# The first layer's 780 pairs in six full row groups, and the last 34 of them stacked three times in the seventh

## The reference

```
x0 = xk = e                                   # (1024, 39, 16)
for W in (f0, f1, f2):                        # (39*39,128), (128*39,128), (128*39,128)
    z = einsum('bfd,bgd->bfgd', x0, xk).reshape(b, f * g, d)
    xk = einsum('bpd,pm->bmd', z, W)          # (b, 128, 16)
    outs.append(xk)
h = concat(sum(concat(outs, 1), -1), dense_ctx)   # (1024, 400)
y = relu(relu(h @ W_top1 + b1) @ W_top2 + b2) @ W_top3
```

## Time and profile before

| | |
|---|---|
| median of 3 runs | 1332.29 us (1331.56 to 1333.27) |
| the profiled execution's own time | 1330.08 us |
| its span, first to last instruction | 1328.3 us |
| mean granted TensorE clock | 0.992 of full speed |
| busy shares PE / DVE / ACT / POOL | 96% / 87% / 69% / 79% |

### The profile page before, as it was taken

The page is one execution under the profiler, slowest core; times in us unless marked ns, Lnnn a source line. Parts: engine busy times, 40 slices in busy tenths (PEclk is TensorE's granted clock), DMA queues, the critical chain, the costliest instruction groups (busy, mean ns, idle before and its releaser), DMA issues. The chain is left out here.

```text
span 1328.3 us, 21624 instructions
## 1 busy us (share of the span) xinstructions
PE 1276.6 (96%) x5983; PEld 1015.4 (76%) x5983; DVE 1155.5 (87%) x3210; ACT 915.7 (69%) x3053; POOL 1050.0 (79%) x743
## 2 busy tenths in 40 slices
PE   4799999999999999999999999999999999999998
PEld 2487777887778777887778877788777877788787
DVE  3499999699988999789996999969999799988983
ACT  2377776577766777677775777757776677767783
POOL 7588888688886888779887788968888688884661
PEclk9799999999999999999999999999999999999999
DMA  7732333322333332223333033331233322223000
GB/s 192 163 58 53 61 64 65 62 38 47 53 62 62 64 58 43 47 52 62 66 64 59 10 64 66 64 62 15 57 64 65 62 54 44 45 57 62 1 3 1
DMA packets 129421, 76.08 MB, mean 57 GB/s; under 512 B 90792, under 2 KB 98201, under 8 KB 129301
## 3 DMA queue, kind: packets, MB, share of 16 engines
q1 hardware_dynamic: 119061, 72.07, 26.6%
q0 software_dynamic: 10240, 2.64, 2.3%
HBM read 68.16 MB, written 3.87 MB: 54 GB/s over the span
## 5 line engine op out<-in xcount | busy, mean ns | idle before, releaser
L392 ACT ACTIVATE parts<-pieces,x_cols 128x128 f32<-128x128 f32 x2560 | 718.1, 377 | 166.1 <-PE pieces L688 164.0
L526 DVE SCALAR_TENSOR_TENSOR parts<-pieces,x_cols,parts 128x128 f32<-128x128 f32 x2432 | 679.4, 340 | 113.2 <-PE pieces L688 92.0
L686 PE MATMUL pieces<-w_hi,cur_hi 128*128 128x512 f32 (+1 forms) x1280 | 548.1, 428 | 22.4 <-DVE parts L526 22.2
L688 PE MATMUL pieces<-w_hi,cur_lo 128*128 128x512 f32 (+1 forms) x1280 | 498.6, 390 | 0.0
L687 PE MATMUL pieces<-w_lo,cur_hi 128*128 128x512 f32 (+1 forms) x1280 | 498.4, 389 | 0.0
L340 POOL TENSOR_TENSOR parts<-parts 128x1024 f32<-128x1024 f32 x127 | 320.3, 2522 | 140.0 <-DVE parts L526 136.8
L331 POOL DMA_INDIRECT emb<-in_table,rows x320 | 342.2, 1069 | 80.8 <-issue 62.1
L686 PEld LDWEIGHTS pieces<-w_hi,cur_hi 128*128 128x128 f32 x1280 | 241.5, 189 | 93.5 <-DVE parts L526 43.8
L411 ACT ACTIVATE pairs_hi<-pairs 117x512 fp32r<-117x512 f32 (+1 forms) x224 | 141.9, 634 | 202.2 <-DVE pairs L536 192.2
L688 PEld LDWEIGHTS pieces<-w_hi,cur_lo 128*128 128x128 f32 x1280 | 240.9, 188 | 51.5
L687 PEld LDWEIGHTS pieces<-w_lo,cur_hi 128*128 128x128 f32 x1280 | 242.0, 189 | 47.7
(11 more groups left out here) (66 smaller groups left out, 596.4 us busy)
## 6 DMA issues: line engine op xcount, KB each, us to landing
partners<-x_wide SPq DMA_DIRECT2D x62, 546.0 KB
partners<-x_wide SPq DMA_DIRECT2D x31, 468.0 KB
x_rep<-x_wide SPq DMA_DIRECT2D x96, 78.0 KB
emb<-in_table,rows POOLq DMA_INDIRECT x320
x_diag<-x_cols SPq DMA_DIRECT2D x256, 10.0 KB
x_wide<-emb SPq DMA_DIRECT2D x32, 80.0 KB
x_wide<-emb SPq DMA_DIRECT2D x32, 32.0 KB
wt<-in_wt SPq DMA_DIRECT2D x1, 1024.0 KB
```

Source lines behind the costliest of these rows:

```text
L392: last = nc.scalar.activation(parts[n % 2][:, 4 * i + r, :], src[:, r * H:(r + 1) * H], ACT.Copy, scale=x_cols[n // 4][:, n % 4, f:f + 1])
L526: nc.vector.scalar_tensor_tensor(acc, src[:, r * H:(r + 1) * H], x_cols[n // 4][:, n % 4, f:f + 1], acc, ALU.mult, ALU.add).then_inc(acc_d ...
L686: nc.tensor.matmul(dst[:, 0:width], hi[:, cols], w1_hi[:, ws], start=True, stop=False)
L688: nc.tensor.matmul(dst[:, 0:width], lo[:, cols], w1_hi[:, ws], start=False, stop=True).then_inc(l2d_ready if q in D_PIECES else l2a_ready, 1)
```

## The change

The pairs are laid out anew. Groups 1 to 6 have all 128 rows: 117 as before (three shifts), and 11 more rows (SPARE) with pairs of fields 0 to 10 of a further shift. That holds 746 different pairs (repeats have zero weights), and 34 are left. They go into a group of 40 rows (10 fields by 4 shifts, with some repeats whose weights are zero), and the 40 rows stand three times in the seventh group (120 rows). In the first 40 rows the operands are the high parts, in the next 40 high pairs by low weights, in the last 40 low pairs by high weights, so one product (L670's place) gives what three gave. For this the seventh group's low-part instruction on DVE becomes a `scalar_tensor_tensor`, which takes the high part away only in rows 80 to 119 by a factor per partition (`take_low`), and the weights of the group are built likewise. The seventh group multiplies by a new tile `x_end`. `load_x` now issues 7 transfers and `load_partners` 7, where each issued 3; the waits count them. The weights come in two transfers, zeros included, where there were five and a memset; `shift_rows` has 128 rows a group.

```diff
@@ -35,14 +35,16 @@
 
 REP = 3
 FX = F + 1
-KPART = REP * F
-
-SHIFTS = F // 2 + 1
-PAIRK = (SHIFTS + REP - 1) // REP
-LAST_ROWS = (SHIFTS - REP * (PAIRK - 1)) * F
+SPARE = P - REP * F
+PAIRK = 7
+FULL = PAIRK - 1
+WHOLE_SHIFTS = REP * FULL
+END_FIELDS, END_SHIFTS = 10, 4
+END = END_FIELDS * END_SHIFTS
+LAST_ROWS = REP * END
 XT_ROWS = 2 * F
 X_STEP = XT_ROWS
-X_LOADS, WIDE_STORES, DIAG_LOADS = 1, 3, BLK_B
+X_LOADS, PARTNER_LOADS, WIDE_STORES, DIAG_LOADS = REP + 1 + REP, REP + 1 + REP, 3, BLK_B
 
 PIECES = 10
...
@@ -81,7 +83,7 @@
 
 
 def rows_of(k):
-    return KPART if k < PAIRK - 1 else LAST_ROWS
+    return P if k < FULL else LAST_ROWS
 
 
 def cin_kernel(nc, t, out):
...
@@ -233,16 +236,9 @@
                 sp.dma_start(part, t["w1"][cols, :].rearrange("(f g) m -> g f m", g=H)).then_inc(w1_loaded, 16)
             sp.dma_start(ident[:], t["ident"]).then_inc(const_loaded, 16)
             sp.dma_start(shift_rows, t["shift_rows"]).then_inc(const_loaded, 16)
-            whole = KPART * (PAIRK - 1)
-            sp.dma_start(w0_raw[:, 0:PAIRK - 1, :],
...
-            sp.dma_start(w0_swapped[:, 1:PAIRK - 1, :], t["w0_swapped"][KPART - F:whole - F, :].rearrange(
-                "(k p) m -> p k m", p=KPART)).then_inc(w0_loaded, 16)
-            sp.dma_start(w0_swapped[0:LAST_ROWS, PAIRK - 1, :], t["w0_swapped"][whole - F:, :]
-                         ).then_inc(w0_loaded, 16)
+            sp.dma_start(take_low[:], t["take_low"]).then_inc(const_loaded, 16)
+            sp.dma_start(w0_raw, t["w0"].rearrange("(k p) m -> p k m", p=P)).then_inc(w0_loaded, 16)
+            sp.dma_start(w0_swapped, t["w0_swapped"].rearrange("(k p) m -> p k m", p=P)).then_inc(w0_loaded, 16)
 
             def store_tile(tile, i):
...
@@ -267,13 +263,25 @@
                 first = x_wide[bass.ds(tile, 1), 0:F, :].rearrange("o r c -> (o r) c")
                 for r in range(REP):
                     sp.dma_start(x_rep[i % 2][r * F:(r + 1) * F, :], first).then_inc(x_rep_loaded[i % 2], 16)
+                sp.dma_start(x_rep[i % 2][REP * F:P, :], first[0:SPARE, :]).then_inc(x_rep_loaded[i % 2], 16)
+                end = first[SPARE:SPARE + 1, :]
+                src = bass.AP(end.tensor, end.offset, [[0, END_SHIFTS], [COLS, END_FIELDS], [1, COLS]])
+                for r in range(REP):
+                    sp.dma_start(x_end[i % 2][r * END:(r + 1) * END, :], src).then_inc(x_rep_loaded[i % 2], 16)
 
             def load_partners(tile, i):
+                flat = x_wide[bass.ds(tile, 1), :, :]
                 for r in range(REP):
-                    steps = len(range(r, SHIFTS, REP))
-                    first = x_wide[bass.ds(tile, 1), r:r + F, :].rearrange("o r c -> (o r) c")
-                    src = bass.AP(first.tensor, first.offset, [[COLS, F], [REP * COLS, steps], [1, COLS]])
-                    sp.dma_start(partners[i % 2][r * F:(r + 1) * F, 0:steps, :], src
+                    src = bass.AP(flat.tensor, flat.offset + r * COLS, [[COLS, F], [REP * COLS, FULL], [1, COLS]])
+                    sp.dma_start(partners[i % 2][r * F:(r + 1) * F, 0:FULL, :], src
+                                 ).then_inc(partners_loaded[i % 2], 16)
+                src = bass.AP(flat.tensor, flat.offset + WHOLE_SHIFTS * COLS,
+                              [[COLS, SPARE], [COLS, FULL], [1, COLS]])
+                sp.dma_start(partners[i % 2][REP * F:P, 0:FULL, :], src).then_inc(partners_loaded[i % 2], 16)
+                src = bass.AP(flat.tensor, flat.offset + (SPARE + WHOLE_SHIFTS) * COLS,
+                              [[COLS, END_SHIFTS], [COLS, END_FIELDS], [1, COLS]])
+                for r in range(REP):
+                    sp.dma_start(partners[i % 2][r * END:(r + 1) * END, FULL, :], src
                                  ).then_inc(partners_loaded[i % 2], 16)
 
...
@@ -459,9 +467,8 @@
                 last = nc.scalar.activation(w1_hi[:, cols], part.rearrange("p f m -> p (f m)"), ACT.Copy)
             last.then_inc(w1_hi_ready, 1)
             act.wait_ge(w0_summed, 1)
-            nc.scalar.activation(w0_hi[:, 0:PAIRK - 1, :], w0_raw[:, 0:PAIRK - 1, :], ACT.Copy)
-            nc.scalar.activation(w0_hi[0:LAST_ROWS, PAIRK - 1, :], w0_raw[0:LAST_ROWS, PAIRK - 1, :], ACT.Copy
-                                 ).then_inc(w0_hi_ready, 1)
+            nc.scalar.activation(w0_hi[:, 0:FULL, :], w0_raw[:, 0:FULL, :], ACT.Copy)
+            nc.scalar.activation(w0_lo[:, FULL, :], w0_raw[:, FULL, :], ACT.Copy).then_inc(w0_hi_ready, 1)
             act.wait_ge(ones_set, TILES)
             copy_x_cols(0, 0)
             for k in range(PAIRK):
...
+                                (tile - i % 2) * 8 * PARTNER_LOADS + i % 2 * 16 * PARTNER_LOADS)
                 wait(dve, pairs_lo_ready, g - 1)
-                nc.vector.tensor_tensor(pairs[buf][0:rows, :], partners[i % 2][0:rows, k, :], x_rep[i % 2][0:rows, :],
+                x = x_rep[i % 2] if k < FULL else x_end[i % 2]
+                nc.vector.tensor_tensor(pairs[buf][0:rows, :], partners[i % 2][0:rows, k, :], x[0:rows, :],
                                         ALU.mult).then_inc(pairs_ready, 1)
 
...
 
             def take_pairs_low(tile, i, k):
                 g, buf, rows = tile * PAIRK + k, (i * PAIRK + k) % 2, rows_of(k)
                 dve.wait_ge(pairs_hi_ready, g + 1)
                 wait(dve, pairs_used, g - 1)
-                nc.vector.tensor_tensor(pairs_lo[buf][0:rows, :], pairs[buf][0:rows, :],
-                                        pairs_hi[buf][0:rows, :].bitcast(FP32), ALU.subtract
-                                        ).then_inc(pairs_lo_ready, 1)
+                if k < FULL:
+                    nc.vector.tensor_tensor(pairs_lo[buf][0:rows, :], pairs[buf][0:rows, :],
+                                            pairs_hi[buf][0:rows, :].bitcast(FP32), ALU.subtract
+                                            ).then_inc(pairs_lo_ready, 1)
+                else:
+                    nc.vector.scalar_tensor_tensor(pairs_lo[buf][0:rows, :], pairs_hi[buf][0:rows, :].bitcast(FP32),
+                                                   take_low[0:rows, 0:1], pairs[buf][0:rows, :], ALU.mult, ALU.add
+                                                   ).then_inc(pairs_lo_ready, 1)
 
             def take_cur1(tile, col, i):
 
...
-            for rows, ks in ((KPART, slice(0, PAIRK - 1)), (LAST_ROWS, slice(PAIRK - 1, PAIRK))):
-                last = nc.vector.tensor_tensor(w0_raw[0:rows, ks, :], w0_raw[0:rows, ks, :], w0_swapped[0:rows, ks, :],
-                                               ALU.add)
-            last.then_inc(w0_summed, 1)
+            dve.wait_ge(w0_loaded, 2 * 16)
+            nc.vector.tensor_tensor(w0_raw, w0_raw, w0_swapped, ALU.add).then_inc(w0_summed, 1)
+            dve.wait_ge(const_loaded, 3 * 16)
             dve.wait_ge(w0_hi_ready, 1)
-            for rows, ks in ((KPART, slice(0, PAIRK - 1)), (LAST_ROWS, slice(PAIRK - 1, PAIRK))):
-                last = nc.vector.tensor_tensor(w0_lo[0:rows, ks, :], w0_raw[0:rows, ks, :],
-                                               w0_hi[0:rows, ks, :].bitcast(FP32), ALU.subtract)
-            last.then_inc(w0_lo_ready, 1)
+            nc.vector.tensor_tensor(w0_lo[:, 0:FULL, :], w0_raw[:, 0:FULL, :], w0_hi[:, 0:FULL, :].bitcast(FP32),
+                                    ALU.subtract)
+            nc.vector.scalar_tensor_tensor(w0_hi[:, FULL, :], w0_lo[:, FULL, :].bitcast(FP32), take_low[:, 1:2],
+                                           w0_raw[:, FULL, :], ALU.mult, ALU.add).then_inc(w0_lo_ready, 1)
             dve.wait_ge(w1_hi_ready, 1)
             for part, cols in w1_raw:
...
@@ -665,8 +676,9 @@
                     wait(pe, cur1_lo_ready, tile)
                     wait(pe, sum1_ready, tile)
                 hi, lo = pairs_hi[buf][0:rows, :], pairs_lo[buf][0:rows, :]
-                nc.tensor.matmul(cur1_bank[:], w0_hi[0:rows, k, :], hi, start=k == 0, stop=False)
-                nc.tensor.matmul(cur1_bank[:], w0_lo[0:rows, k, :], hi, start=False, stop=False)
+                if k < FULL:
+                    nc.tensor.matmul(cur1_bank[:], w0_hi[0:rows, k, :], hi, start=k == 0, stop=False)
+                    nc.tensor.matmul(cur1_bank[:], w0_lo[0:rows, k, :], hi, start=False, stop=False)
                 nc.tensor.matmul(cur1_bank[:], w0_hi[0:rows, k, :], lo, start=False, stop=k == PAIRK - 1
                                  ).then_inc(pairs_used, 1)
 
...
@@ -828,8 +840,27 @@
 
     i = np.arange(F)
     w0 = np.asarray(inputs["L0_rec_f0"])
-    rows = np.concatenate([i * F + (i + s) % F for s in range(SHIFTS)])
-    swapped = np.concatenate([(i + s) % F * F + i for s in range(1, SHIFTS)])
+    one, two = np.full((PAIRK, P), -1), np.full((PAIRK, P), -1)
+    for k in range(FULL):
+        one[k] = np.arange(P) % F
+        two[k] = one[k] + np.where(np.arange(P) < REP * F, REP * k + np.arange(P) // F, WHOLE_SHIFTS + k)
+    end = np.arange(LAST_ROWS) % END
```

(16 more changed lines are left out.)

48 lines of the change are left out of this document (21 added, 27 removed).

## The result

The changed kernel takes 1348.62 us in the median of four runs (1344.0 to 1350.48), where the kernel before takes 1332.39 beside it (1331.56 to 1333.27). The ratio is 1.0115, with a 95% interval of 1.0096 to 1.0134: slower by about 1%, where I forecast 1327.9 us and a small gain. The profiled execution took 1344.0 us with a span of 1342.2, against 1330.08 and 1328.3, at a mean granted clock of 0.988 against 0.992. So the trace shows 13.9 us of loss; the other three executions were longer by 3.4 to 6.5 us than the one that was profiled, and of those there is no trace.

What follows compares the result with a forecast made beforehand. PE was taken as bound from late in A through B, DVE through C, D and half the next A. Terms -9.1 + 1.0 + 3.7 = -4.4 us gave 1327.9 us, range 1321.5 to 1335.5.

Steps and rivals of the forecast that it cites:

- What bounds the kernel: Reading of steady state: PE sets the pace late in A through B, DVE through C, D and half the next A.
- A: First stretch of a four-stretch quad, 42.75 us, with extra PE layers; forecast 0.46 us shorter, seven times.
- B: Second stretch of a quad, 43.20 us, with extra PE layers; forecast 0.46 us shorter, seven times.
- C: Third stretch of a quad, 35.97 us, without extra PE layers; two fewer products forecast to save 0.27 us, seven times.
- D: Fourth stretch of a quad, 36.71 us, where DVE never waits for PE; two fewer products forecast to save 0.
- Part 1: Seventh group on PE: two fewer products a tile free 0.46 us, counted only where DVE waits; 9.1 us off.
- Part 2: Seventh group's low part on DVE: three-operand instruction estimated at 0.74 us, 0.06 more than now; 1.0 us on.
- second rival: Three-operand instruction on DVE streams at half rate: 0.53 us more each time, 1336.9 us in all; 15%.
- Part 3: Transfers in steady state: more bytes and eight more SP issues, 3.2 us, covered by early issue; no cost.
- Part 4: Start, where DVE waits for tile 2's partners: extra queued transfers and bytes delay them; 3.7 us on, bounds 1.2 to 5.5.
- Rival 3: POOL's folds meet other DVE instructions: one more meeting a quad gives 1336 us, one less 1320; 8% and 6%.

Runs made afterwards that it cites:

- g1: The kernel before with POOL's first fold of a block halved (4 slices added, not 8): 1286.77 us, ratio 0.9666 to before.
- g4: The kernel before with the seventh group's two products left out only for tiles prepared in the second stretch of a quad: 1333.18 us, ratio 1.0015.
- e2: The kernel before with the seventh group's low part taken by the three-operand instruction (factor -1), nothing else changed: 1333.37 us, ratio 1.0007.
- g2: The kernel before with POOL's first fold halved and the seventh group's two products left out: 1272.47 us, ratio 0.956.
- e3: The changed kernel's layout and transfers, but with all three seventh-group products and the two-operand low-part instruction: 1339.35 us, ratio 1.0056.
- h1: The changed kernel with x_end and the seventh group's partner transfers issued behind the large partner transfers, on their own semaphores: 1338.96 us, ratio 1.0047.
- g3: The changed kernel with x_end's transfers on a semaphore of their own, so PE's first products don't wait for them: 1345.78 us, ratio 1.0101.
- i1: The kernel before with the third fold of a block moved from POOL to DVE: 1370.05 us, ratio 1.0285.
- e4: The changed kernel with the old two-operand instruction for the seventh group's low part: 1343.2 us, ratio 1.0077.
- j1: The kernel before with DVE's pairs and low parts and the products moved to other slots, past the folds: 1351.03 us, ratio 1.0146.

## Why the prediction was wrong

**What bounds the kernel.** Which waits stand in DVE's timeline, and that A and B end on PE, was read rightly. "DVE [sets the pace] from there through C, D and the first half of the next A" was the step that failed. I took 98% and 99% of busy time as DVE's own work. In D 4.27 of the 36.26 us are port wait, and g1, where it is 1.01, shows what is left: 34.63 us, set by PE. The bound of C and D is a loop of two engines. The fourth fold of each stretch waits for DVE, the other three come out of POOL's own queue behind it, and the folds block DVE.

**Part 1, two products.** The term was -9.1 us. The 0.46 us a tile is right: g1 and g2 differ by 31 times that. B's allotment is right too (-0.52 measured). A's 0.46 is wrong (+0.57), although its products do lie between waits for PE: the saving there was outweighed by 1.19 us more port wait at A's beginning. C's 0.27 and D's 0 are wrong (+0.27, +0.26); g4 shows one of these directly, B's 0.46 costing C 0.60. The error of the step was to count the missing work only where DVE waits for PE, and to take the rest of the schedule as fixed.

**Part 2, the three-operand instruction.** Right: 741 ns for the estimated 740, and +0.8 us in e2 for my 1.0, though e2's interval takes in no change, so it doesn't confirm the second. The second rival falls with it. The rule of the Trainium skill cited there, half throughput for a `scalar_tensor_tensor` with two SBUF sources that aren't bf16, does not hold here: 512 float32 elements took 63 ns more than in the two-operand form (737 for 674 in e2), and not some 530 ns.

**Part 3, transfers in steady state.** Right: e3's quad is 158.63 us, as before's.

**Part 4, the start.** The place and mechanism were right, the size was not: 3.7 us predicted (bounds 1.2 to 5.5), 7.59 measured at the end of the first stretch. What was mis-sized: I had the partners 1.5 us later on the queue, and they were issued 6.6 us later. `x_rep` of tile 2 was issued 1.66 us later, the four issues behind it took 3.6 us with their pauses and not 1.5, and SP paused 1.4 us more ahead of the partners. h1 attributes 4.3 us to that order. I also wrote of the earlier trace rows that PE runs dry there; it was busy for 4.63 of the 6.00 us. That the delay of the first products vanishes in DVE's wait was right (g3).

**Rival 3.** The mechanism that decided was the one given 8% on the bad side. Its price of 1.0 us a quad for one more meeting stands beside 0.58 - (-1.07) = 1.65 measured. "In C and D both engines follow DVE, so their pattern should stay as it is" was the argument against it, and it is refuted: they follow DVE, but DVE's place in its own work follows PE, from whose end B hands over to C.

Added up for the profiled execution: steady state +6.4 us over 30 stretches and not -8.1, the start +7.6 and not +3.7; 14.0 and not -4.4.

**What stays open.** That DVE's port wait makes up C and D is counted, but why the wait settles at 3.3 and 4.3 us is only argued: no sum of one engine's work gives 36.24 us, g1 shortened POOL's work together with the port wait, and the run that cut the port wait by moving a fold (i1) was limited by something else. Why C gives back more (0.60) than B gains (0.46) isn't explained. The executions of the changed kernel spread by 6.5 us. One more meeting lengthens a D stretch from 37.0 to 37.9 us: in the changed kernel's trace, its fastest execution, it happens in one of seven D, in h1's, its slowest, in six. That fits the spread, but the slowest execution of the changed kernel was not traced, so it is not shown that this is its cause. Against the runs of before beside them e4 is 10.6 us longer and the changed kernel 16.2; of the 5.6 between them the three-operand form explains 0.8. h1's median, 6.9 us above before, is better than the changed kernel's by more than the 4.3 us that its start gives.

## What to carry to other kernels

A busy share near 100% does not say that an engine's own work is the bound: compare each instruction's duration with its shortest one of the same shape, and subtract. Where two engines can block each other, a saving on a third one shifts who meets whom, and its price has either sign; here one and the same edit gave 14.3 us or cost 3.4, by the length of a fold on another engine. And where a critical load sits in a queue, new small transfers belong behind it.

## What the hardware showed that was not expected

- A pair product 0.01 us from the fold's start got through in 0.68 us and lengthened the fold by 0.55 (2.95 for 2.40); one 0.30 us later was held for 1.96 us. Over all traces the line is sharp: no pair product or low part that began up to 0.03 us behind a fold's start took over 1 us, and every one that began 0.07 to 0.15 us behind it did. The held ones ended some 0.55 us after the fold. Two of DVE's in a row can hold a fold: in j1, at 272.52 us, a pair product began 0.22 us ahead of a fold, the low part right behind it at 273.12 took 0.68 us as well, and the fold took 3.32.
- What was held has two tensors in SBUF. L533, with one in PSUM, took 1.12 us for four inside a fold, as outside.
- The three `x_end` transfers, 80 KB each, occupied SP's queue for 0.70 us each at the start; those of `x_rep`, 78 KB, 0.38. That the source of `x_end` has repeated rows is not shown to be the reason: the seventh group's partner transfers, 80 KB without repeats, took 0.61 us in the median, `x_end` 0.66.
- A three-operand instruction with two float32 tensors in SBUF took 741 ns for 512 elements. Against L533's 341 ns for 128, which reads one tensor from PSUM, that is 1.04 ns an element, the rate of the two-operand form; this is an estimate, since only one size was measured.
